# A first quarter of attention maxima entered by matrix products with diagonal blocks, 18 pairs of maxima ahead instead of 22, and two groups of rows transposed inside the first unit

## The reference

```
x = x + layernorm(attn(layernorm(x)))
  q, k, v = xn @ W + b            (16 heads of 64)
  q = q / sqrt(64)
  out = softmax(q @ k.T) @ v      (per head and batch, 2048 x 2048)
  return out @ Wo + bo
x = x + layernorm(ffn(layernorm(x)))
```

## Time and profile before

| what | value |
|---|---|
| median of the runs shown | 2386.46 us |
| the profiled execution, its own time | 2388.58 us |
| its span, first to last instruction | 2386.7 us |
| outside the span | 1.88 us |
| busy share of TensorE (PE), GpSimd (POOL), VectorE (DVE), ScalarE (ACT) | 98%, 88%, 85%, 59% |
| granted TensorE clock, mean | 0.992 |

### The profile page before, as it was taken

The page is one execution under the profiler, slowest core; times in us unless marked ns, Lnnn a source line. Parts: engine busy times, 40 slices in busy tenths (PEclk is TensorE's granted clock), DMA queues, the critical chain, the costliest instruction groups (busy, mean ns, idle before and its releaser), DMA issues.

```text
span 2386.7 us, 43553 instructions
## 1 busy us (share of the span) xinstructions
PE 2348.6 (98%) x15628; PEld 1178.0 (49%) x15628; DVE 2035.4 (85%) x3208; ACT 1415.4 (59%) x1671; POOL 2107.2 (88%) x1206
## 2 busy tenths in 40 slices
PE   6999999999999999999999999999999999999998
PEld 3455454545445454454545445454544545444454
DVE  7888888888888888888888888888888888888877
ACT  5656556566565656656565655656656565655646
POOL 5888989888898989989888898989989888899986
PEclk8999999999999999999999999999999999999999
DMA  1100001000000000100001000100000000110101
GB/s 51 29 14 28 28 15 33 28 15 28 28 20 28 28 15 28 34 15 27 28 16 32 28 19 23 33 23 20 28 27 20 28 28 15 35 30 21 37 27 36
DMA packets 62969, 62.55 MB, mean 26 GB/s; under 512 B 28868, under 2 KB 46660, under 8 KB 62756
## 3 DMA queue, kind: packets, MB, share of 16 engines
q1 hardware_dynamic: 61748, 59.44, 8.5%
q10 hardware_dynamic: 1008, 0.33, 0.1%
HBM read 56.88 MB, written 2.61 MB: 25 GB/s over the span
## 4 chain that ended last, share of the span: by engine, by line
PE 94%; DVE 2%; POOL 1%; DMA 1%; ACT 1%; issue 1%; SPq 0%; POOLq 0%; DVEq 0%; ACTq 0%
PE o_ps L442 37%; PE spare_ps L401 14%; PE score_ps L421 10%; PE score_ps L427 10%; PE score_ps L424 10%; PE spare_ps L387 3%; PE spare_ps L487 3%; PE spare_ps L378 3%; PE spare_ps L369 3%; PE spare_ps L454 1%; DVE max_part L867 1%; POOL total L1142 1%; DMA m_all<-m_scratch 0%; DVE ln_stats L835 0%; PE spare_ps L467 0%
## 5 line engine op out<-in xcount | busy, mean ns | idle before, releaser
L1142 POOL TENSOR_TENSOR total<-total,probs 128x832 f32<-128x832 f32 (+1 forms) x896 | 1761.0, 1965 | 232.6 <-ACT probs L691 161.1
L867 DVE TENSOR_REDUCE max_part<-spare_ps 128x1 f32<-128x512 f32 x2027 | 1303.6, 685 | 295.3 <-PE spare_ps L401 276.7
L691 ACT ACTIVATE probs<-score_ps 128x1024 f32<-128x1024 f32 x1024 | 999.2, 1021 | 785.4 <-PE score_ps L427 784.2
L442 PE MATMUL o_ps<-probs,v_sb 128*64 128x512 f32 x4096 | 977.2, 598 | 0.0
L442 PEld LDWEIGHTS o_ps<-probs,v_sb 128*64 128x64 f32 x4096 | 268.3, 136 | 434.7 <-issue 282.5
L401 PE MATMUL spare_ps<-k_hi,q_hi 64*128 64x512 f32 x2027 | 466.2, 454 | 6.9 <-DVE max_part L867 3.2
L401 PEld LDWEIGHTS spare_ps<-k_hi,q_hi 64*128 64x128 f32 x2027 | 195.2, 184 | 436.8 <-issue 262.1
L421 PE MATMUL score_ps<-q_hi,kd_hi 64*128 64x512 f32 x2048 | 406.9, 393 | 0.9 <-ACT score_ps L681 0.9
L427 PE MATMUL score_ps<-q_hi,kd_lo 64*128 64x512 f32 x2048 | 405.2, 392 | 0.0
L424 PE MATMUL score_ps<-q_lo,kd_hi 64*128 64x512 f32 x2048 | 403.8, 390 | 0.0
L903 DVE TENSOR_REDUCE part_sum<-probs 128x192 f32<-128x768 f32 (+1 forms) x255 | 392.4, 1539 | 0.8 <-ACT probs L691 0.7
(11 more groups left out here) (136 smaller groups left out, 1118.5 us busy)
## 6 DMA issues: line engine op xcount, KB each, us to landing
m_all<-m_scratch SPq DMA_DIRECT2D x64, 512.0 KB, 4.4
denom<-denom_scratch SPq DMA_DIRECT2D x122, 128.0 KB, 2.9
m_scratch<-neg_rows SPq DMA_DIRECT2D x256, 1.0 KB
y_acc<-in_L_attn_x SPq DMA_DIRECT2D x8, 256.0 KB, 6.6
key_f<-in_L_attn_x SPq DMA_DIRECT2D x8, 256.0 KB, 2.8
block_out<-probs SPq DMA_DIRECT2D x8, 256.0 KB, 2.3
denom_col<-denom SPq DMA_DIRECT2D x61, 4.0 KB
denom_scratch<-denom_col SPq DMA_DIRECT2D x61, 4.0 KB, 1.4
```

The lines of the kernel that those rows point to most:

```text
L442: last = nc.tensor.matmul(o_ps[half(h), :], v_sb[:, b, kt, half(h)], probs[:, st % RING, h, :], start=(kt == 0), stop=(kt == T - 1))
L691: nc.scalar.activation(probs[:, st % RING], score_ps[st % 2][:], ACT.Exp, scale=SCALE).then_inc(s["exp_done"], 1)
L867: nc.vector.reduce_max(max_part[:, G % 2, h, qt, kc:kc + 1], bank[max_bank(n, h)], AX.X).then_inc(s["max_done"], 1)
L1142: nc.gpsimd.tensor_tensor(others(total[:, G % 2], G), so_far, others(probs[:, st % RING], G), ALU.add).then_inc(s["sum_done"], 1)
```

## The change

Five things are changed together.

- The first chunk's seed is no longer written to DRAM, read back and copied by ACT. `m_all` is filled with diagonal blocks: block t of head h has the negated maxima of 128 queries on its diagonal. DVE makes the four blocks of head 0 in one instruction, ACT those of head 1 in four. TensorE multiplies a matrix of ones with them (`first_seed`), once for each of the two score tiles, so that each partition gets the row of maxima.
- 18 pairs instead of 22 run before the first double. Doubles 1 to 3 issue three pairs where they had two, and double 0 three, all behind its scores. From double 4 on the lead is 22 again.
- Row groups 6 and 7 are normalised by ACT in doubles 1 and 2 and transposed in doubles 3 and 4, in spare banks.
- In the start, the fourth part of the keys is projected after pair 8 instead of pair 6, and DVE takes the first values after pair 11 instead of pair 16.
- The counts of the semaphores for the DRAM trip of the later chunks are shifted by one.

```diff
-LEAD = 22
+LEAD, FIRST = 22, 18
+LATE_X = {3: 6, 4: 7}
+def maxima_from(n):
+    return min(FIRST + 3 * n, LEAD + 2 * n, STEPS)
+def maxima_in(n):
+    return range(maxima_from(n), maxima_from(n + 1))
...
-        FIRST_LATE_X = {13: 4, 15: 5, 17: 6, 18: 7}
-        FIRST_MAX_BANKS = [("r0", "r1"), ("s00", "s01")] * (T // 2 + 1) + [("s10", "s11"), ("r0", "r1"), ("o", "r2"), ("r0", "r1")]
+        FIRST_LATE_X = {13: 4, 15: 5}
+        FIRST_MAX_BANKS = [("r0", "r1"), ("s00", "s01")] * (T // 2) + [("r0", "r1"), ("o", "r2")]
+        FIRST_V_DONE = 11
...
+            def first_seed(self, st):
+                self.pe.wait_ge(s["diag_done"], 2)
+                for h in range(2):
+                    ps = self.take(f"s{st}{h}", None, 0)
+                    for k in range(2):
+                        last = nc.tensor.matmul(ps[half(k), :], ones[:], m_all[:, h, :], start=True, stop=True)
+                last.then_inc(s["seed_done"], 1)
...
-                if 2 * n + LEAD < STEPS:
-                    me.max_pair(2 * n + LEAD)
+                for m in maxima_in(n)[:1] if n else []:
+                    me.max_pair(m)
+                if n == 0:
+                    me.first_seed(0)
                 me.scores(2 * n)
+                if n == 0:
+                    me.first_seed(1)
                 me.scores(2 * n + 1)
-                if 2 * n + LEAD < STEPS:
-                    me.max_pair(2 * n + LEAD + 1)
+                for m in maxima_in(n)[1 if n else 0:]:
+                    me.max_pair(m)
...
+                if n in LATE_X:
+                    me.transpose_x(LATE_X[n])
...
+        def act_diag(act):
+            act.wait_ge(s["neg_max_done"], 1)
+            act.wait_ge(s["const_ready"], 1)
+            for t in range(TC):
+                ins = nc.scalar.activation(m_all[:, 1, t * P:(t + 1) * P], ident[:], ACT.Copy, scale=neg_max[:, 0, TC + t:TC + t + 1])
+            ins.then_inc(s["diag_done"], 1)
...
+        def dve_diag(dve):
+            dve.wait_ge(s["neg_max_done"], 1)
+            dve.wait_ge(s["const_ready"], 1)
+            nc.vector.tensor_tensor(m_all[:, 0, :].rearrange("p (t n) -> p t n", t=TC), ident[:].unsqueeze(1).to_broadcast([P, TC, P]),
+                                    neg_max[:, 0, 0:TC].unsqueeze(2).to_broadcast([P, TC, P]), ALU.mult).then_inc(s["diag_done"], 1)
```

More of the change, by code:

```diff
@@ L124, in spare_banks @@
         G, u, c, d = n // PER_CHUNK, n // (PER_CHUNK * NC), n // PER_CHUNK % NC, n % PER_CHUNK
-        for st in (2 * n + LEAD, 2 * n + LEAD + 1):
-            for h in range(2 if st < STEPS else 0):
-                use("max", 2 * st + h)
+        for m in maxima_in(n):
+            for h in range(2):
+                use("max", 2 * m + h)
         if keys_at(u, c, d):
@@ L561, in pe_program @@
             me.transpose_x(3)
-            me.max_pair(6)
-            me.project_k(0, 3, FIRST_K_BANK[3])
-            for n in range(7, LEAD):
+            for n in range(6, FIRST):
                 me.max_pair(n)
                 if n == 8:
+                    me.project_k(0, 3, FIRST_K_BANK[3])
+                if n == 9:
                     me.project_q(1, FIRST_Q_BANK[1])
@@ L1048, in dve_program @@
                 dve_x_statistics(dve, g)
-            for n in range(LEAD):
+            for n in range(FIRST):
                 for h in range(2):
@@ L1057, in dve_program @@
                 G, u, c, d = n // PER_CHUNK, n // (PER_CHUNK * NC), n // PER_CHUNK % NC, n % PER_CHUNK
-                more = 2 * n + LEAD < STEPS
-                if more:
-                    dve_max(dve, 2 * n + LEAD, 0)
-                    dve_max(dve, 2 * n + LEAD, 1)
+                for m in maxima_in(n)[:1]:
+                    dve_max(dve, m, 0)
+                    dve_max(dve, m, 1)
                 for g in ffn_at(n, LOW):
@@ L1069, in dve_program @@
                     dve_recip(dve, G - 1)
-                if more:
-                    dve_max(dve, 2 * n + LEAD + 1, 0)
-                    dve_max(dve, 2 * n + LEAD + 1, 1)
+                for m in maxima_in(n)[1:]:
+                    dve_max(dve, m, 0)
+                    dve_max(dve, m, 1)
                 if d == NEG_MAX_AT and G + 1 < CHUNKS:
```

53 lines of the change are left out of this document (26 added, 27 removed).

## The result

| | before | after |
|---|---|---|
| median, lowest, highest of 7 runs each | 2387.06, 2386.04, 2388.25 us | 2393.49, 2392.51, 2396.98 us |
| ratio of the runs | | 1.0027, interval 1.0018 to 1.0037 |
| span of the profiled execution | 2386.7 us | 2391.9 us |
| granted clock, mean | 0.992 | 0.994 |

What follows compares the result with a forecast made beforehand. The prediction took TensorE to bound the kernel, and DVE its start. Double 1 opening 1.2 us earlier and doubles 1 to 4 costing 5.4 more gave +4.2 on the 2386.46 median: 2390.7 us, range 2385.5 to 2394.5.

Steps and rivals of the forecast that it cites:

- the prediction's own sign of being wrong: Granted clock 0.50 between 49 and 55 us would show a second fall and the forecast wrong.
- The maxima: First chunk's negated maxima on DVE: 0.8 us earlier, at 37.5 instead of 38.28; 36.5 without the clock's fall.
- The seed: TensorE starts it at 39.4; both seeds and steps take 7.4 us, double 0's scores through at 46.8, 3.3 us earlier.
- The rest of double 0: From last scores to double 1: three pairs waiting on banks take 4.5 us instead of 2.4; double 1 at 51.3.
- Doubles 1 to 4: Moved pairs cost 1.5 us in each of doubles 1 to 3, two transposes 1.0 more: 5.4 us in sum.
- this fall as a rival: Clock falls again in double 0 and 1, losing 1.5 to 2.5 us: 2392.2 to 2393.2 us; chance 0.25.
- From double 5 to the end: Both kernels issue the same from double 5 on, so its shift, +4.2 us, carries to the end.
- the first term of the sum: Start up to the opening of double 1: 1.2 us earlier than before, entered as -1.2.
- Waits hidden: Second pairs in double 0 and doubles 1 to 4 start 0.23 us behind the first: 2384.5 us; chance 0.10.
- Clock up: No falls at 25 and 35 us: 2387.5 with waits, chance 0.10; 2381.3 with hidden waits, chance 0.05.
- Late seed: Diagonal block or group 5 late, seed starts after 41: up to 2 us more, 2392.7 us; chance 0.05.
- rival A: Rival set for the experiments: the seed's products are what costs; no chance given.

Runs made afterwards that it cites:

- late edit: Kernel before, with double 488's two products with the values issued before its second pair of maxima instead of behind the transposes: 2387.70 us, ratio 1.0001.
- seed alone: Kernel before with only the seed changed to diagonal blocks and eight products, still 22 pairs ahead and two pairs a double: 2392.92 us, ratio 1.0026.
- the start's order alone: Kernel before with only the start's order changed as in the changed kernel, still 22 pairs and the seed through DRAM: 2388.26 us, ratio 1.0002.
- the waits filled: Changed kernel with two idle TensorE products behind each of the first two of double 0's three pairs: 2392.45 us, ratio 1.0021.
- apart, rounded and filled: Changed kernel with third pairs moved away from second ones, seeds as two rounded products, and idle products in the start: 2388.55 us, ratio 1.0003.

## Why the prediction was right where it was, and where it was not

The time is inside the range, and most terms of the sum were met. But the prediction's own sign of being wrong, a clock of 0.50 between 49 and 55, came too.

| what | forecast | measured |
|---|---|---|
| negated maxima | 37.5 | 37.24 |
| TensorE starts the seed | 39.4 | 38.79 |
| double 0's scores are through | 46.8 | 46.91 |
| double 1 opens | 51.3 | 51.54 |
| double 5, against before | +4.2 | +5.6 |
| end, against before | +4.2 | +5.2 (span), +6.4 (medians) |

**The maxima.** Forecast 37.5, and 36.5 if the clock does not fall at 25; measured 37.24. The clock did not fall, and the whole start was 0.69 us later (first reductions at 17.09, before 16.40): 36.5 + 0.7 = 37.2. So the number was met by luck: the branch that I gave less chance, in a start that began later, comes out at the same place. Whether the clock falls at 25 is not a matter of the order: each order ran with and without it. What the order itself gives up to the negated maxima is 0.2 to 0.6 us (20.36 and 20.78 against 20.15), not 0.8. Of the hole of 2.52 about half was the lower clock's: without the fall it is 1.01 (late edit) and 1.44 (seed alone). The run with the start's order alone shows no gain.

**The seed.** Forecast 39.4, measured 38.79: the maxima came 0.26 earlier, and ACT's four blocks took 1.28, not 1.64. Forecast 7.4 us for seeds and scores, measured 8.1 (38.79 to 46.91); the fall at 34 and the return at 44 came about where I took them. Last scores 46.9, forecast 46.8: here two misses cancel.

**The rest of double 0.** Forecast 4.5, measured 4.63; waits of 0.88. Double 1 at 51.54, forecast 51.3: 0.24 of the miss stands by then.

**Doubles 1 to 4.** Forecast +5.4, measured +6.56 (25.00 from the opener of double 1 to that of double 5, before 18.44). By doubles: double 2 took 7.12 instead of 5.65, +1.47, forecast 1.5. Double 3 5.95 instead of 3.91, +2.04: 1.46 and a transpose of 0.58, forecast 0.5. Double 4 4.50 instead of 4.01, +0.49. Double 1 7.43 instead of 4.87, +2.56: 1.16 more than the 1.4 of its pair. **This is the step that failed**: from double 1's opener to the end of its scores it took 2.90 us at the lower clock (51.54 to 54.44), the same stretch of double 2 1.74 (58.97 to 60.71). I had this fall as a rival with a chance of 0.25, and it came on top of the forecast. I priced it at 1.5 to 2.5; it cost 1.16 in the trace, and its removal (the run with the waits filled) brought 1.20 in double 1. With it, the sum is -0.95 + 6.56 = +5.6 at double 5, where it was measured.

The sign against it was in my own text: the stretch after the scores had as little work as that before 35 us, where the clock had fallen. The Trainium skill, "TensorE: Matmul & The Clock Gate", section "A second HAM failure mode: psum-queue depth-cycling", says that cycling through banks makes short idles at which the clock swings; the windows of after from 44 to 54 us agree (1.00, then 0.50), and in the run with filled waits the clock stayed at 1.00 from 44 us on.

**From double 5 to the end.** The shift went from 5.6 to 5.2 in the profiled spans. The medians say 6.4, with an interval of 4.3 to 8.8 us. The profiled execution of before was slow for its kernel, 1.5 us above the median, and it is one with the fall at 25 us; against the same start without that fall (the run with the late edit) the shift at double 5 is 6.4. So the first term of the sum took for a gain of the change what was a slow start of one execution, and the two figures of 6.4 fit. How often the kernel before falls at 25 when it is not profiled is not known, so this is likely but not shown. The forecast was also added to a median of 2386.46, which is 2387.06 over all seven runs: 0.6 of the 2.8 us of the miss.

Two of after's seven runs were 3 us above the others at a granted clock of 0.993 and 0.992 instead of 0.994 or more. A fall at the late wait, at 2224 to 2233 us, left up to 2.3 us at the end where it was seen; for those two runs there is no trace, so this is not shown.

**The rivals.** Waits hidden: excluded by five waits of 0.88. Clock up: true at 25, not at 34. Late seed: no, 38.79. That the products themselves cost (rival A): in part. They bring double 0's scores no earlier than the trip through DRAM does with the shorter lead, and with 22 pairs they are pure addition. Rounded and halved in number they give 2.0 us by the medians, 1.5 in the trace.

## What to carry to other kernels

Count the banks before moving pairs together: a group that takes two banks of three waits for its reader every time, here 0.88 us a pair, and placing the pairs apart gave back 4.5 us by the medians. Where an engine waits in a stretch anyway, ask first which clock level it is at: idle products laid in the waits, not in front of something that is due, gave 3.8 us by the medians and 2.5 in the trace on the kernel before, more than any form of the new seed that was run. And compare a start by its distance from a common landmark, and in more than one execution: one execution's lower clock made a reordering look worth 1.7 us that was worth 0.2 to 0.6.

## What the runs showed of the hardware

- The first reductions begin between 16.34 and 17.26 us in thirteen profiled executions, without relation to the kernel. In four of them the granted clock was lower at 25 to 28 us (0.50, 0.50, 0.61, 0.71). Leaving out the one with idle products at that place, these four are among the six earliest (16.34 to 16.61), and with a beginning at 16.86 or later it never fell. Counted from the first reductions, the negated maxima came 1.1 to 1.8 us later with the fall than without it, in either order.
- The same DVE subtraction before the wait at 2224 us (`v_split`, 32x512) took 0.96 us in the profile of before, 1.22 with the late edit and 1.56 to 1.65 in the other eleven. In all thirteen it ends 0.53 to 0.56 us behind the end of GpSimd's product with `denom`: the earlier in that product it starts, the longer it takes. That it waits for GpSimd is how I read this; no run moved that product.
- A seed as four full-precision products takes 3.68 us at the lower and 1.94 at the upper clock, as two rounded products 1.22 and 0.73 (the latter in the run apart, rounded and filled).
- Two idle products of 384 columns take 0.8 us of TensorE's time. Ten groups of 192 to 448 columns kept the granted clock at 1.00 to 56 us, where in the same order without them it was 0.50 from 35 to 50.
